# k's mixes: the first product of each moved from VectorE to ScalarE, two behind each sigmoid of r's units 4 and 5

## The chip, the cores and the metric

The kernel runs on the 8 NeuronCores of one Trainium2 chip. Each core takes 1024 of the 8192 tokens (two sequences of 4096, four chunks each), with a lane of 128 tokens ahead of its chunk, and computes all 2048 channels of them. The cores exchange nothing. The metric is the device time of the slowest core, in microseconds.

## The reference, cut to what matters

The layer normalises x, mixes each token with the one before it in four ways, multiplies the mixes by four matrices, runs a recurrence over tokens, multiplies by Wo, normalises again and gates with a second projection whose weights are rounded to -1, 0 or 1.

```python
prev = jnp.concatenate([x[:, 1:2, :], x[:, :-1, :]], axis=1)
xx = prev - x
xk = x + xx * tm_k        # xv, xr, xg likewise
r = xr @ Wr.T;  k = xk @ Wk.T;  v = xv @ Wv.T
g = sigmoid(xg @ Wg.T)
wkv = _wkv_scan(k, v, exp(-exp(time_decay)), time_first)
o = sigmoid(r) * wkv * g @ Wo.T
s = layernorm(o) * ln_g + ln_b
return xn + s * silu(ffn(xn))
```

A mix is computed as xn(now) * (1 - tm) + xn(before) * tm. "The first product" below is xn(now) * (1 - tm); the second instruction multiplies xn(before) by tm and adds the first product.

## The kernel before

Channels lie on partitions, in 16 groups of 128, and tokens along the free axis. `xn` (f16, 16 groups) is the normalised input. `mova` and `movb` (bf16) hold mixes: r's mix is in `mova` first, k's goes into `movb`, and v's overwrites r's in `mova`. A matrix comes in eight units of 256 output channels, loaded into the slots R0, R1, R2, X0 and X1.

Nothing is scheduled automatically. The class `Program` keeps one queue for each engine, written in the order of the code, and each engine runs its queue strictly in that order. `P.op` gives back a token; a later operation that is passed this token waits for it. So what stands ahead in a queue and waits delays all that is behind it in that queue.

The place of the change is the passage from r to k and v:

- TensorE works through r's units 4 and 5 (`unit_tile`, eight tiles of 16 matmuls, 512 columns each), then through units 6 and 7 with the 16 channel groups in the outer loop: for each group `ic`, eight matmuls go into the eight PSUM banks (`bk`). Then come k and v in turns, tile by tile: three tiles of k for one group of output channels, three tiles of v, and so on.
- The counter `turn` is set to 4 ahead of units 4 and 5. Their eight tiles therefore use the banks 4, 5, 6, 7, 0, 1, 2, 3, and the eight accumulations of units 6 and 7 use the same banks in the same order. The first round of units 6 and 7 (`ic` 0) needs each bank emptied: its eighth matmul goes into bank 3, which holds the eighth tile of units 4 and 5.
- ScalarE empties the banks with sigmoids (`sr_evict`), after it has done the sigmoids of r's first four units and two small exponentials.
- VectorE makes k's 16 mixes (`t_kb`), and then v's 16 (`t_va`). A mix over 1152 tokens is two instructions in `lerp`: a TENSOR_SCALAR into the buffer `lu` (two of them, in turns), and a SCALAR_TENSOR_TENSOR out of it. The mix of group `ic` for v may not start before units 6 and 7 have read that group of `mova` (`t_ic[ic]`).
- The first matmul of k waits for all of `t_kb`, the first matmul of v for all of `t_va`.

An existing helper, `lerp_pair`, makes r's mixes with the first product on ScalarE, in pieces of 512 or 256 tokens with four buffers.

Of the kernel before, what the change touches and what calls it, by code (L numbers as in the profile page):

```python
# [9 lines left out]
AF = mybir.ActivationFunctionType  # L10
OP = mybir.AluOpType
# [10 lines left out]
T_ALL = LANE + T_OWN  # L22
# [3 lines left out]
TMK, TMV, TMR, TMG = 0, 1, 2, 3  # L26
# [75 lines left out]
def build_nc():  # L102
    nc = bass.Bass("TRN2", target_bir_lowering=False)
    P = Program(nc)
# [21 lines left out]
    def at(name, shape, dtype, offset):  # L126
        return nc.alloc_sbuf_tensor_at(name, shape, dtype, offset=offset)

    xn = at("xn", [128, CH, 1154], F16, XN)
    mova = at("mova", [128, CH, T_ALL], BF16, A)  # L130
    movb = at("movb", [128, CH, T_ALL], BF16, B)
# [11 lines left out]
    lu = [at("lu0", [128, T_ALL], F16, SMALL), at("lu1", [128, T_ALL], F16, ROWS + 20736)]  # L143
# [26 lines left out]
    def sm(name, n, dtype=F32):  # L170
        nonlocal small
        t = at(name, [128, n], dtype, small)
        small += -(-n * (2 if dtype == F16 else 4) // 32) * 32
        return t
    vec = sm("vec_sb", 161)
    ident = vec[:, 97:161].bitcast(F16)
    om = sm("om", 64)
# [147 lines left out]
    def lerp(dst, ic, tm, col, n, *tokens):  # L325
        k = lu_n[0] % 2
        lu_n[0] += 1
        u = lu[k]
        P.op("DVE", lambda e: e.tensor_scalar(u[:, 0:n], xn[:, ic, col:col + n],
                                              om[:, 16 * tm + ic:16 * tm + ic + 1], None, OP.mult),  # L330
             *tokens)
        return P.op("DVE", lambda e: e.scalar_tensor_tensor(  # L332
            dst, xn[:, ic, col - 1:col - 1 + n], vec[:, 16 * tm + ic:16 * tm + ic + 1], u[:, 0:n],
            OP.mult, OP.add), drain=True)
# [4 lines left out]
    def lerp_pair(dst, ic, tm, col, n, *tokens):  # L339
# [9 lines left out]
            OP.mult, OP.add), t_u, *tokens)  # L349
        return lq_free[k]  # L350


    stg_free = [None] * 6
    nstg = [0]
# [28 lines left out]
    def unit_tile(mat, u, oc, mov, t0, n, *tokens):  # L383

        slot = have[(mat, u)]
        b = next_bank()
        for ic in range(CH):
            tok = mm(ps[b][:, 0:n], unit[slot][:, ic, 128 * oc:128 * oc + 128],
                     mov[:, ic, t0:t0 + n], ic == 0, ic == CH - 1,
                     have[(mat, u, ic // 8)], bank_free[b], *(tokens if ic == 0 else ()),  # L390
                     signal=ic == CH - 1)
        return b, tok


    def sr_evict(b, och, t0, n, tok, c0=0):
        bank_free[b] = P.op("ACT", lambda e: e.activation(
            att[:, och, t0:t0 + n], ps[b][:, c0:c0 + n], AF.Sigmoid), tok)
# [36 lines left out]
    t_om = P.op("DVE", lambda e: e.tensor_scalar(om[:, :], vec[:, 0:64], -1.0, 1.0, OP.mult, OP.add), t_vec)  # L434
# [157 lines left out]
    t_head = [t_xn[(0, 0)], t_xn[(0, 1)], t_xh[(0, 1)]] + xh_free  # L592
    stg_free[1] = t_grp[7]


    t_kb = [lerp(movb[:, ic, :], ic, TMK, 2, T_ALL, *t_head) for ic in range(16)]

    rslot = {3: "X0", 4: "X1", 5: "R0", 6: "R1", 7: "X0"}
    turn[0] = 4
# [3 lines left out]
    for u in (4, 5):  # L603
        for oc in range(2):
            for h in range(2):
                b, tok = unit_tile("wr", u, oc, mova, 512 * h, 512)
                sr_evict(b, 2 * u + oc, 512 * h, 512, tok)
        slot_free[rslot[u]] = tok
    kslot = [("R0", "R2", "R1")[n % 3] for n in range(16)]

# [7 lines left out]
    t_va = []  # L618
    t_ic = []
# [10 lines left out]
    t_rend = t_grp[7]  # L630

    for ic in range(16):
        t_va.append(lerp(mova[:, ic, :], ic, TMV, 2, T_ALL, t_ic[ic]))


    P.op("DVE", lambda e: e.memset(za[:, 0:1], 0.0), t_rend)
# [450 lines left out]
```

How the kernel before makes its waits and increments, by code:

```python
        def run(e):  # L60
            for s, n in todo:
                e.wait_ge(s, n)
            if drain:
                e.drain()
            ins = emit(e)
            if signal:
                ins.then_inc(self.sem[eng], 1)
# [13 lines left out]
        def run(e):  # L81
            for s, v in todo:
                e.wait_ge(s, v)
            if accum_op == OP.bypass:
                e.dma_start(out, in_).then_inc(sem, 16)
            else:
                e.dma_start(out, in_, accum_op=accum_op).then_inc(sem, 16)
# [7 lines left out]
        def run(e):  # L95
            for s, v in todo:
                e.wait_ge(s, v)
```

## Time and profile before

| | us |
|---|---|
| Median of 3 runs (lowest, highest) | 743.63 (743.05, 745.22) |
| The profiled execution's own time | 743.03 |
| Its span on the slowest core (all cores: 739.7 to 741.3) | 741.3 |
| Outside the span | 1.7 |
| TensorE busy in the span | 706.4 (95%) |
| VectorE busy | 465.9 (63%) |
| ScalarE busy | 241.3 (33%) |
| Mean granted TensorE clock, share of full | 0.995 to 0.997 |

The table reads so: TensorE is at work nearly all the time, and the times of the eight cores lie within 1.6 us of each other. The other two engines have a good deal of idle time, averaged over the span, which says nothing yet of any one stretch.

### The profile page before, as it was taken

How to read it: one execution, taken by the hardware profiler on the slowest of the kernel's cores; microseconds unless marked ns; L12 is line 12 of the kernel's file. 1: busy time of each engine (PE TensorE's matmuls, PEld its weight loads, DVE VectorE, ACT ScalarE, POOL GpSimd, SP SyncE). 2: the span in 40 equal slices, each digit the busy share in tenths (PEclk: the TensorE clock that was granted, in tenths of full speed). 3: DMA queues.
4: the chain of work that ended last, by engine and by line, in shares of the span. 5: the costliest groups of instructions: out<-in, count | busy, mean ns of one | idle time of the engine just before them, and what ended most of it. 6: DMA issues, size and time to landing. Idle time of an engine off the chain costs nothing.

```text
span 741.3 us, 10313 instructions; the slowest of 8 cores (739.7 to 741.3 us)
## 1 busy us (share of the span) xinstructions
PE 706.4 (95%) x3809; PEld 372.0 (50%) x3852; DVE 465.9 (63%) x580; ACT 241.3 (33%) x344; POOL 123.8 (17%) x156
## 2 busy tenths in 40 slices
PE   1889999999999999999999999999999999999994
PEld 1447644456666666666665444444444444444441
DVE  6777589957777677776789496674111110566565
ACT  4766751043444234442126654412111110000000
POOL 1010101001010010100000000112134410876710
PEclk9999999999999999999999999999999999999997
DMA  8988194444783958739317933894999975356643
GB/s 237 172 222 171 30 212 85 73 114 90 195 152 95 225 117 209 144 93 217 65 51 199 334 108 78 185 168 36 138 176 149 171 149 158 86 142 156 185 113 113
DMA packets 22372, 107.71 MB, mean 145 GB/s; under 512 B 2482, under 2 KB 2610, under 8 KB 14898
## 3 DMA queue, kind: packets, MB, share of 16 engines
q0 software_dynamic: 12672, 50.34, 41.1%
q1 hardware_dynamic: 9648, 56.71, 24.5%
q8 instruction: 31, 0.51, 0.3%
q14 instruction: 17, 0.14, 0.1%
q10 hardware_dynamic: 4, 0.02, 0.0%
HBM read 140.61 MB, written 8.39 MB: 201 GB/s over the span
## 4 chain that ended last, share of the span: by engine, by line
PE 83%; DVEq 5%; DMA 5%; DVE 4%; issue 1%; ACT 1%; POOL 0%; ACTq 0%; SPq 0%; POOLq 0%
PE ps L380 83%; DVEq L64 5%; DVE movb L332 3%; DMA wR<-wr 3%; DMA xs<-x 2%; PE ps L290 1%; DVE mova L332 0%; DVE zt L966 0%; ACT xh L268 0%; DVE bst L245 0%; DVE ps L960 0%; POOL wR L85 0%; DVE xn L317 0%; ACT raw L400 0%; DVE bst L952 0%
## 5 line engine op out<-in xcount | busy, mean ns | idle before, releaser
L380 PE MATMUL ps<-mova,wR 128*128 128x384 bf16 (+2 forms) x1555 | 283.4, 340 | 5.2 <-DMA wR<-wr 3.0
L380 PEld LDWEIGHTS ps<-mova,wR 128*128 128x128 bf16 x1568 | 152.6, 98 | 130.3 <-issue 7.7
L380 PE MATMUL ps<-movb,wR 128*128 128x384 bf16 x768 | 127.4, 326 | 0.0
L380 PE MATMUL ps<-wo,att 128*128 128x512 bf16 x502 | 110.1, 379 | 0.5
L380 PE MATMUL ps<-wq,xn 128*128 128x512 bf16 x501 | 109.9, 379 | 0.7
L380 PEld LDWEIGHTS ps<-movb,wR 128*128 128x128 bf16 x768 | 75.1, 98 | 49.7
L380 PEld LDWEIGHTS ps<-wo,att 128*128 128x128 bf16 x512 | 50.1, 98 | 60.4
L380 PEld LDWEIGHTS ps<-wq,xn 128*128 128x128 f16 x512 | 50.0, 98 | 60.5 <-issue 0.3
L868 DVE TENSOR_TENSOR att<-sg,att 128x512 bf16<-128x512 bf16 x32 | 15.2, 475 | 96.1 <-ACT sg L866 96.1
L711 DVE TENSOR_TENSOR kv<-ps,ek 128x384 f32<-128x384 f32 x48 | 26.6, 557 | 51.4 <-PE ps L380 47.9
L952 DVE BATCH_NORM_STATS2 bst<-ps 128x6 f32<-128x512 f32 x32 | 21.4, 691 | 46.4 <-PE ps L380 46.4
L866 ACT ACTIVATE sg<-ps 128x512 bf16<-128x512 f32 x32 | 19.1, 597 | 87.3 <-PE ps L380 87.3
L332 DVE SCALAR_TENSOR_TENSOR mova<-xn,vec_sb,lu 128x1152 bf16<-128x1152 f16 (+2 forms) x33 | 44.0, 1333 | 3.1
L645 ACT ACTIVATE ek<-ps,hb 128x128 f32<-128x128 f32 x16 | 5.9, 367 | 120.2 <-PE ps L380 120.2
L380 PE MATMUL ps<-mova,wX 128*128 128x512 bf16 x186 | 43.9, 379 | 0.3
L657 DVE TENSOR_TENSOR_SCAN zb<-w_sb,ek 128x1152 f32<-128x1152 f32 x16 | 40.9, 2559 | 1.5
L672 DVE TENSOR_TENSOR_SCAN za<-w_sb,kv 128x1152 f32<-128x1152 f32 x16 | 40.9, 2559 | 1.4
L702 ACT ACTIVATE wq<-stg,nmag 128x2048 bf16<-128x2048 f32 x16 | 31.4, 1996 | 21.5 <-DVE stg L700 21.5
L776 DVE SCALAR_TENSOR_TENSOR ps<-ps,nscale,bias 128x512 f32<-128x512 f32 x32 | 24.2, 757 | 20.5 <-PE ps L380 19.2
L85 POOL DMA_DIRECT2D wR<-wv x16 | 8.5, 536 | 157.4 <-PE ps L380 157.4
L955 ACT ACTIVATE sd<-mv,eps 128x1 f32<-128x1 f32 x8 | 2.4, 294 | 93.4 <-DVE mv L954 93.4
L780 ACT ACTIVATE g<-ps 128x512 bf16<-128x512 f32 x32 | 18.7, 597 | 39.7 <-DVE ps L776 39.5
(83 smaller groups left out, 638.9 us busy)
## 6 DMA issues: line engine op xcount, KB each, us to landing
stg<-wf SPq DMA_DIRECT2D x32, 1024.0 KB, 9.1
xs<-x SPq DMA_DIRECT2D x9, 1024.0 KB, 9.3
wR<-wk POOLq DMA_DIRECT2D x16, 512.0 KB, 11.0
wR<-wv POOLq DMA_DIRECT2D x16, 512.0 KB, 10.7
wo<-wo POOLq DMA_DIRECT2D x16, 512.0 KB, 23.7
y<-zt SPq DMA_DIRECT2D x7, 1024.0 KB, 7.2
wR<-wg POOLq DMA_DIRECT2D x12, 512.0 KB, 17.2
stg<-x POOLq DMA_DIRECT2D x6, 1024.0 KB, 9.4
```

What stands on the lines that cost most here:

```text
L64: e.drain()
L332: return P.op("DVE", lambda e: e.scalar_tensor_tensor(dst, xn[:, ic, col - 1:col - 1 + n], vec[:, 16 * tm + ic:16 * tm + ic + 1], u[:, 0:n ...
L380: return P.op("PE", lambda e: e.matmul(bank, w_ap, m_ap, start=first, stop=last), *tokens, signal=signal)
L657: P.op("DVE", lambda e: e.tensor_tensor_scan(zb[:, 1:1 + T_ALL], wb, ek[m][:, :], 0.0, OP.mult, OP.add), t_weu, drain=True)
L672: P.op("DVE", lambda e: e.tensor_tensor_scan(za[:, 1:1 + T_ALL], wb, kv[:, :], 0.0, OP.mult, OP.add), drain=True)
L702: t_wq[(s, q)] = P.op("ACT", lambda e: e.activation(dst, stg[i][:, :], AF.Sign, bias=nmag[:, 0:1]), t, t_nmag, wq_free[s % 2], *tokens)
L711: bank_free[b] = P.op("DVE", lambda e, j=j, b=b: e.tensor_tensor(kv[:, 384 * j:384 * j + 384], ps[b][:, 0:384], ek[m][:, 384 * j:384 * j + ...
L776: t = P.op("DVE", lambda e: e.scalar_tensor_tensor(ps[b][:, :], ps[b][:, :], nscale[:, 0:1], bias[s % 2][:, :], OP.mult, OP.add), tok, t_b ...
L780: bank_free[b] = P.op("ACT", lambda e: e.activation(g2[s][:, tb, :], ps[b][:, :], AF.Silu), t, t_att[15] if s >= 2 else None)
L866: t = P.op("ACT", lambda e: e.activation(sg[k][:, :], ps[b][:, :], AF.Sigmoid), tok, sg_free[k])
L868: sg_free[k] = P.op("DVE", lambda e: e.tensor_tensor(att[:, och, 512 * h:512 * h + 512], sg[k][:, :], att[:, och, 512 * h:512 * h + 512], ...
L952: P.op("DVE", lambda e, s=s: e.bn_stats(bst[m][:, 6 * s:6 * s + 6], ps[banks[s]][:, :]), toks[s])
```

## The change

A new helper `lerp_wide` makes a mix over all 1152 tokens with its first product on ScalarE (an ACTIVATE Copy with a scale per partition) and its second instruction on VectorE. It uses the whole of both `lu` buffers, in turns by `ic % 2`; the first product of group `ic` waits until VectorE has finished the mix of group `ic - 2`. The first two of k's mixes are written ahead of units 4 and 5; the other fourteen stand in pairs behind the first seven of the eight sigmoids of units 4 and 5. v's first mix waits, in addition, until both buffers are free.

```diff
+    lw_free = [None] * 2
+
+    def lerp_wide(dst, ic, tm, *tokens):
+
+        k = ic % 2
+        t_u = P.op("ACT", lambda e: e.activation(lu[k][:, :], xn[:, ic, 2:2 + T_ALL], AF.Copy,
+                                                 scale=om[:, 16 * tm + ic:16 * tm + ic + 1]),
+                   t_om, lw_free[k], *tokens)
+        lw_free[k] = P.op("DVE", lambda e: e.scalar_tensor_tensor(
+            dst, xn[:, ic, 1:1 + T_ALL], vec[:, 16 * tm + ic:16 * tm + ic + 1], lu[k][:, :],
+            OP.mult, OP.add), t_u, *tokens)
+        return lw_free[k]
...
-    t_kb = [lerp(movb[:, ic, :], ic, TMK, 2, T_ALL, *t_head) for ic in range(16)]
+    t_kb = [lerp_wide(movb[:, ic, :], ic, TMK, *t_head) for ic in range(2)]
...
                 sr_evict(b, 2 * u + oc, 512 * h, 512, tok)
+                for ic in range(len(t_kb), min(len(t_kb) + 2, 16)):
+                    t_kb.append(lerp_wide(movb[:, ic, :], ic, TMK))
...
     for ic in range(16):
-        t_va.append(lerp(mova[:, ic, :], ic, TMV, 2, T_ALL, t_ic[ic]))
+        t_va.append(lerp(mova[:, ic, :], ic, TMV, 2, T_ALL, t_ic[ic], *(lw_free if ic == 0 else ())))
```

On ScalarE, in the kernel before, the last small exponential (into `eu_sb`) is followed directly by the sigmoids that empty the banks of units 4 and 5, one bank (`ps4`, `ps5`, ...) after the other; the number behind `ps` is the bank:

```order
L591 ACTIVATE eu_sb_123<-vec_sb_120 128x16
L396 ACTIVATE att_46<-ps4 128x512 [waits done_PE]
L396 ACTIVATE att_46<-ps5 128x512 [waits done_PE]
L396 ACTIVATE att_46<-ps6 128x512 [waits done_PE]
L396 ACTIVATE att_46<-ps7 128x512 [waits done_PE]
```

In the changed kernel two first products (L357, into `lu0` and `lu1`) stand between each two of them. These are the last rows of the eight, up to the sigmoid of bank 3, which is the eighth; the sigmoid of `ps4` behind it is already one of units 6 and 7:

```order
L357 ACTIVATE lu0_62<-xn_43,om_121 128x1152 [waits done_DVE]
L357 ACTIVATE lu1_63<-xn_43,om_121 128x1152 [waits done_DVE]
L409 ACTIVATE att_46<-ps2 128x512 [waits done_PE]
L357 ACTIVATE lu0_62<-xn_43,om_121 128x1152 [waits done_DVE]
L357 ACTIVATE lu1_63<-xn_43,om_121 128x1152 [waits done_DVE]
L409 ACTIVATE att_46<-ps3 128x512 [waits done_PE]
L409 ACTIVATE att_46<-ps4 128x512 [waits done_PE]
```

All sixteen first products of k now stand ahead of the sigmoid of bank 3 in ScalarE's queue, and each of them but the first two waits for VectorE.

On VectorE, at the end of k's mixes and the start of v's, the kernel before has pairs without waits on another engine:

```order
L329 TENSOR_SCALAR lu_62<-xn,om 128x1152
L332 SCALAR_TENSOR_TENSOR movb<-xn,vec_sb,lu_62 128x1152
L329 TENSOR_SCALAR lu_63<-xn,om 128x1152
L332 SCALAR_TENSOR_TENSOR movb<-xn,vec_sb,lu_63 128x1152
L329 TENSOR_SCALAR lu_62<-xn,om 128x1152 [waits done_PE]
```

In the changed kernel the second instructions of k (L360) are alone and wait for ScalarE, and v's first mix also waits for VectorE's own last one:

```order
L360 SCALAR_TENSOR_TENSOR movb<-xn,vec_sb,lu_62 128x1152 [waits done_ACT]
L360 SCALAR_TENSOR_TENSOR movb<-xn,vec_sb,lu_63 128x1152 [waits done_ACT]
L329 TENSOR_SCALAR lu_62<-xn,om 128x1152 [waits done_PE,done_DVE]
L332 SCALAR_TENSOR_TENSOR mova<-xn,vec_sb,lu_62 128x1152
L329 TENSOR_SCALAR lu_63<-xn,om 128x1152 [waits done_PE]
```

Sixteen instructions have left VectorE's queue here. TensorE's, GpSimd's and the DMA queues hold the same instructions in the same order as before.

## Rows read from the trace of the kernel before

**Rows 1.** TensorE's waits over the span: engine, line waited for, total us, times, longest.

```profile
PE ps L380 <- DVE zb L637: 0.5, 1, 0.5
```

**Rows 2.** Chain that ended last, in order of time: start us, us, what.

```profile
156.05 1.42 DVE mova L332
157.61 210.76 PE ps L380 x1296
```

**Rows 3.** Timeline of VectorE, 95 to 157 us: start, us, instruction, idle before it.

```profile
95.22 0.52 DVE L329 TENSOR_SCALAR lu<-xn,om 128x1152 f16<-128x1152 f16 x1 [0.18 <-DVE xn L317]
...
97.16 0.51 DVE L329 TENSOR_SCALAR lu<-xn,om 128x1152 f16<-128x1152 f16 x1
...
124.99 1.42 DVE L332 SCALAR_TENSOR_TENSOR movb<-xn,vec_sb,lu 128x1152 bf16<-128x1152 f16 x1
126.33 0.52 DVE L329 TENSOR_SCALAR lu<-xn,om 128x1152 f16<-128x1152 f16 x1
...
156.05 1.42 DVE L332 SCALAR_TENSOR_TENSOR mova<-xn,vec_sb,lu 128x1152 bf16<-128x1152 f16 x1
```

**Rows 4.** Timeline of ScalarE, 100 to 122 us.

```profile
100.39 0.20 ACT L591 ACTIVATE eu_sb<-vec_sb 128x16 f32<-128x16 f32 x1
100.60 1.28 ACT L396 ACT_TABLE_LOAD   x1
101.90 1.08 ACT L396 ACTIVATE att<-ps 128x512 bf16<-128x512 f32 x2
104.55 0.60 ACT L396 ACTIVATE att<-ps 128x512 bf16<-128x512 f32 x1 [1.56 <-PE ps L380]
...
121.81 0.60 ACT L396 ACTIVATE att<-ps 128x512 bf16<-128x512 f32 x1 [2.86 <-PE ps L380]
```

**Rows 5.** Timeline of TensorE, 122 to 158 us.

```profile
122.42 1.03 PE L380 MATMUL ps<-mova,wX 128*128 128x512 bf16 x4
...
149.18 7.96 PE L380 MATMUL ps<-movb,wR 128*128 128x384 bf16 x48
157.61 7.64 PE L380 MATMUL ps<-mova,wR 128*128 128x384 bf16 x46 [0.47 <-DVE zb L637]
```

**Rows 6.** ScalarE's groups of instructions by shape: busy us, mean ns of one.

```profile
L663 ACT ACTIVATE ek<-ek 128x1024 f32<-128x1024 f32 x16 | 16.9, 1058 | 1.3
...
L344 ACT ACTIVATE lu<-xn,om 128x256 f16<-128x256 f16 x32 | 13.2, 497 | 2.8 <-DVE xn L317 2.8
...
L344 ACT ACTIVATE lu<-xn,om 128x512 f16<-128x512 f16 x15 | 9.4, 709 | 3.6 <-DVE xn L317 3.6
L268 ACT ACTIVATE xh<-xs,nm,rs 128x1024 f16<-128x1024 f32 x6 | 7.1, 1233 | 2.1 <-DVE nm L263 1.3 <-DVE om L434 0.7
...
L226 ACT ACT_TABLE_LOAD x1 | 1.3, 1283 | 1.7 <-DVE ones L225 1.7
```

**Rows 7.** Timeline of ScalarE: two series of one instruction, back to back.

```profile
75.73 5.68 ACT L344 ACTIVATE lu<-xn,om 128x256 f16<-128x256 f16 x14
...
147.93 4.03 ACT L396 ACTIVATE att<-ps 128x512 bf16<-128x512 f32 x8 [25.52 <-PE ps L380]
```

**Rows 8.** Timelines: hand-overs between VectorE and ScalarE, and from ScalarE to TensorE.

```profile
34.08 0.69 DVE L317 COPY xn<-ps 128x1024 f16<-128x1024 f16 x1
34.86 3.79 ACT L344 ACTIVATE lu<-xn,om 128x512 f16<-128x512 f16 x6 [2.78 <-DVE xn L317]
35.75 2.74 DVE L347 SCALAR_TENSOR_TENSOR mova<-xn,vec_sb,lu 128x512 bf16<-128x512 f16 x4 [0.99 <-ACT lu L344]
...
55.40 0.59 ACT L400 ACTIVATE raw<-ps 128x512 f32<-128x512 f32 x1
...
56.13 4.09 PE L380 MATMUL ps<-mova,wR 128*128 128x256 bf16 x34 [0.22 <-ACT raw L400]
```

**Rows 9.** Busy time by stretch (PE, PEld, DVE, ACT, POOL), granted clock, DMA share.

```profile
121.00:157.00 36.00, 35.84 (x177) 17.33 (x178) 34.29 (x37) 7.04 (x13) 3.58 (x6) 1.00 0.52 85
```

**Rows 10.** Timeline of TensorE after its longest wait before 93 us.

```profile
46.17 3.61 PE L380 MATMUL ps<-mova,wR 128*128 128x512 bf16 x16 [1.81 <-DMA wR<-wr]
```

## The prediction

> **What bounds the kernel now.** I read TensorE's waits first, because it is busy for 706.4 of 741.3 us. The line that matters is the only one that names the mixes of k and v: TensorE waits once for VectorE there, 0.5 us in all [rows 1]. Then the chain that ended last, and here a reader has to be careful. It runs through VectorE's mixes up to 157.47 us and then through TensorE for 210 us without a break [rows 2], which looks as if all 62 us of mixes set the time. But the timeline of TensorE shows it at work beside them: units 6 and 7 from before 122.42, k from 149.18 to 157.14, and only then a gap of 0.47 us before v's first matmul at 157.61 [rows 5]. In the stretch from 121 to 157 us it is busy for 35.84 of 36.00 us at a granted clock of 1.00, the 2.4 GHz level [rows 9]. So the most that any speeding up of these mixes can give is 0.47 us; what it can cost is not limited like that. VectorE needs 1.94 us for a mix (95.22 to 97.16) and is through with k at 126.41 and with v at 157.47 [rows 3]. ScalarE empties a bank every 3.45 us and idles between: it waits 2.86 us for TensorE ahead of the eighth sigmoid, which runs from 121.81 to 122.41 [rows 4].
>
> **The change part by part.**
>
> *What goes from VectorE.* Sixteen TENSOR_SCALAR of 0.52 us, which start 0.61 ahead of their partners: k's mixes would take 1.34 us each instead of 1.94 (a following instruction starts 1.34 after a SCALAR_TENSOR_TENSOR of 1.42, 124.99 to 126.33 [rows 3]), 9.6 us less, if ScalarE kept up.
>
> *What comes to ScalarE.* A Copy over 1152 elements has no row. The same instruction takes 709 ns for 512 elements and 497 ns for 256 [rows 6], 0.83 ns for each further one, so 1.24 us for 1152. From both sides: the shortest 1024-element row (1.058) gives 1.16 with 128 elements more, the longest (1.233, an ACTIVATE with per-partition operands) 1.34. I take 1.24, since it is the same form. One back to back with the next starts 0.095 before the end: fourteen of 497 ns take 5.68, so 0.399 apart; for sigmoids it is (4.03 - 0.60) / 7 = 0.49 apart [rows 7].
>
> *The hand-overs.* VectorE's copy ends at 34.77 and ScalarE starts at 34.86: 0.09. That product ends at 35.57 and VectorE starts at 35.75: 0.18. ScalarE's eviction ends at 55.99 and TensorE's matmul starts at 56.13: 0.14 [rows 8]. For the bounds I give both of the first two the lower or the higher value. With two buffers, a product waits for the mix two back. So from one product to the second after it there are at least 1.24 + 0.18 + 1.42 + 0.09 = 2.93 us. ScalarE's own work for a pair and a sigmoid is 2 x 1.145 + 0.49 = 2.78, VectorE's 2 x 1.34 = 2.68. The loop through both buffers is the longest: a pair takes 2.93 us.
>
> *ScalarE's queue, step by step.* It is free at 100.60, where the load of the sigmoid's table now stands [rows 4]. Products 0 and 1 start at 100.60 and 101.74; the second ends at 102.98. The table load then puts the first sigmoid 1.30 later (100.60 to 101.90 in [rows 4]), at 104.29. Product 2 starts at 104.78 and 3 at 105.92. The mix of 2 starts at 106.20 and that of 3 behind it at 107.54, to 108.96, so product 5 starts at 109.05. Five loops of 2.93 take product 15 to 123.70. The eighth sigmoid is behind it: 124.85 to 125.45. No other sigmoid is late for anybody: the seventh stands one pair earlier, ends at about 122.5 with bank 2, and TensorE wants that bank at 122.85.
>
> *Who waits for the eighth sigmoid.* It empties bank 3. Units 6 and 7 write the banks in turn, and the row at 122.42 holds the fifth to eighth matmul of their first round, 0.217 apart [rows 5]: the eighth starts at 122.42 + 3 x 0.217 = 123.07. Now the bank is free only at 125.45, and with 0.14 of hand-over the matmul starts at 125.59. Behind it, in TensorE's own order, stands everything else. **TensorE stalls for 2.52 us**, where it did not before.
>
> *What gives some of it back.* k's mixes end at about 126.6 (product 15 ends at 124.94, 0.18 of hand-over, 1.42, and a little queueing behind the mix before). v's first then starts 0.18 later, because it waits for VectorE's own last result, as the first one of k does [rows 3]: 126.8 against 126.33. v's mixes follow 1.94 apart and end at 157.9 instead of 157.47; they gain nothing, because k's are paced by ScalarE. But TensorE now comes to v at 157.14 + 2.52 = 159.66, so the 0.47 us wait goes, with 1.7 us to spare. The matmuls of units 6 and 7, 1.73 us a group, run ahead of v's mixes as before. The 9.6 us taken off VectorE turn into waits of VectorE for ScalarE.
>
> *The sum.* 2.52 - 0.47 = **+2.05 us**. Behind this point the chain is TensorE alone [rows 2], so nothing absorbs it. On the profiled execution's own 743.03 it gives 745.1; the median of the three runs lies 0.60 above that execution, and on it I predict **745.7**. By the bounds: with 1.16 and 0.09 twice the loop is 2.76, the eighth sigmoid ends at 124.2, and the sum is +0.8. With 1.34 and 0.18 twice the loop is 3.12, the sigmoid ends at 126.9, and the sum is +3.5.
>
> *A page weighed against a row.* What the table load costs decides when everything behind it starts, and rows show 1.30 us from its start to that of the sigmoid. The Trainium skill, "ScalarE: Activation LUTs", section "What ACT_TABLE_LOAD costs", puts a switch at about 2.66 us, the load and a drain of about 1.38. By that page the sum would be about +3.4; this trace disagrees with it at this very load, 1.30.
>
> **The rivals.**
>
> 1. *No stall; only the gain.* If the first products are so quick that the eighth sigmoid is done by 122.93, the 0.47 us wait goes for nothing: 743.2. The backlog would have to be 2.5 us shorter over seven pairs, 2.57 us a pair, which is under VectorE's own 2.68. The rows speak against it.
>
> 2. *A shorter or longer stall by the price of the product.* 744.4 at the low bound, 747.1 at the high one; from +2.2 on it counts as slower.
>
> 3. *The load is followed by a wait until the long products have drained.* Before the load there were tiny instructions in this place. A second 1.30 us, the load's own length once more, makes +3.35: 747.0. This is what the page named above would have; the rows speak against it.
>
> 4. *TensorE's clock falls in the stall.* After its wait of 1.81 us it ran sixteen matmuls in 3.61 us, 0.215 apart, at the full level [rows 10], but it has no wait of 2.5 us behind such a busy stretch. If the granted clock went to 1.2 GHz for as long as those sixteen take, they would need 3.5 us more: 749.2. The point from which it decides is a stall longer than the one that the rows show to be harmless.
>
> 5. *Each product loads a table of its own, and each sigmoid loads its table again.* Two loads of 1.30 for each pair: the eighth sigmoid some 18 to 20 us later, 764. Against it: r's mixes did 47 such Copies among square roots, and the only load in that stretch is the one at the start [rows 6]. The Trainium skill, in the same page's section on table sets, says that a copy is in every set, and the trace agrees: no load among those 47.
>
> **How the numbers follow.** The forecast, a stall that makes +1.4 to +2.8, gets 0.62. A longer one (+2.8 to +3.7) gets 0.15, a shorter one (+0.5 to +1.4) 0.12, no stall 0.05, and the drain, the clock and the reloads 0.02 each. A measurement of this kernel can tell about 0.3% from no change, 2.23 us or 745.86. That line lies just above my forecast. Of the forecast's 0.62 I put 0.26 above it; with 0.15 and 0.06 that is 0.47 for slower. Nothing in this stretch has 2.2 us to give, so faster gets 0.01; the rest, 0.52, is the same. The range is 744.1 to 747.3: the two bounds, 0.3 us wider on each side since single runs of the kernel differ by more than 2 us, and it leaves out no stall, the clock and the reloads.
>
> **What would show it.** In the changed profile: ScalarE busy without pause from 94 to about 125.4 us; products of 1.24 us; a pair every 2.93; exactly one table load between 100 and 148; TensorE's wait of 2.5 us for ScalarE, in the row that starts at about 125.6, within the first round of units 6 and 7; no wait ahead of v; VectorE's mixes of k with waits for ScalarE, and v's starting at 126.8. I am wrong if the eighth sigmoid ends before 123 us (products much cheaper than 1.16), if the granted clock is under 1.00 after the stall, or if TensorE waits at k or v again.

## The result, and the profile after

| | us |
|---|---|
| Kernel before, median (lowest) | 743.92 (743.05) |
| Changed kernel, median (lowest) | 746.38 (745.91) |
| Ratio, 95% interval | 1.0036 (1.0026 to 1.0046) |
| Profiled execution after: own time, span on core 5 | 746.6, 745.0 |
| Spans of the cores after | 741.4 to 745.0 |

The kernel is slower by 0.36% in the ratio, 2.46 us between the medians; forecast were 745.7 and +2.05. (Executions in which one die ran at a lower clock throughout, one of the changed kernel's eight, count in the medians but not in the ratios, nor where cores are counted below.)

TensorE's waits in the changed kernel, on its slowest core, are these; against [rows 1], the wait for VectorE is gone and one for ScalarE has come:

```profile
PE ps L393 <- DMA wR<-wr: 3.2, 2, 2.4
PE ps L393 <- ACT att L409: 2.1, 1, 2.1
```

The timeline of ScalarE in the changed kernel answers to [rows 4]. Products and sigmoids follow one another without idle time, with one table load:

```profile
100.88 0.20 ACT L604 ACTIVATE eu_sb<-vec_sb 128x16 f32<-128x16 f32 x1
100.98 2.40 ACT L357 ACTIVATE lu<-xn,om 128x1152 f16<-128x1152 f16 x2
103.40 1.28 ACT L409 ACT_TABLE_LOAD   x1
104.69 0.60 ACT L409 ACTIVATE att<-ps 128x512 bf16<-128x512 f32 x1
105.19 2.39 ACT L357 ACTIVATE lu<-xn,om 128x1152 f16<-128x1152 f16 x2
107.48 0.58 ACT L409 ACTIVATE att<-ps 128x512 bf16<-128x512 f32 x1
108.05 2.58 ACT L357 ACTIVATE lu<-xn,om 128x1152 f16<-128x1152 f16 x2
110.54 0.58 ACT L409 ACTIVATE att<-ps 128x512 bf16<-128x512 f32 x1
...
122.67 2.48 ACT L357 ACTIVATE lu<-xn,om 128x1152 f16<-128x1152 f16 x2
125.06 0.58 ACT L409 ACTIVATE att<-ps 128x512 bf16<-128x512 f32 x1
```

The timeline of TensorE on the same core answers to [rows 5]; its first row, from an earlier stage, is used further down:

```profile
46.66 3.61 PE L393 MATMUL ps<-mova,wR 128*128 128x512 bf16 x16 [2.35 <-DMA wR<-wr]
...
122.91 0.81 PE L393 MATMUL ps<-mova,wX 128*128 128x512 bf16 x3
125.78 0.38 PE L393 MATMUL ps<-mova,wX 128*128 128x512 bf16 x1 [2.06 <-ACT att L409]
126.00 1.02 PE L393 MATMUL ps<-mova,wR 128*128 128x512 bf16 x4
126.86 1.68 PE L393 MATMUL ps<-mova,wX 128*128 128x512 bf16 x4
128.33 1.91 PE L393 MATMUL ps<-mova,wR 128*128 128x512 bf16 x4
130.04 1.26 PE L393 MATMUL ps<-mova,wX 128*128 128x512 bf16 x4
131.14 1.03 PE L393 MATMUL ps<-mova,wR 128*128 128x512 bf16 x4
...
153.58 7.96 PE L393 MATMUL ps<-movb,wR 128*128 128x384 bf16 x48
161.38 7.96 PE L393 MATMUL ps<-mova,wR 128*128 128x384 bf16 x48
```

Two losses are to be seen. The first is the predicted one: the row at 122.42 held four matmuls before; at 122.91 there are three, and the fourth, due at 122.91 + 3 x 0.217 = 123.56, starts at 125.78. That is 2.22 us. The second I had not reckoned with: four matmuls that took 0.86 us from start to start (126.00 to 126.86) take 1.71 a little later (128.33 to 130.04), 0.43 us each, which is half the rate. The stretches of this core show the granted clock of it (the third number from the end):

```profile
121.00:126.00 5.00, 2.94 (x14) 1.18 (x13) 4.73 (x4) 4.61 (x5) 2.12 (x4) 1.00 0.10 13
126.00:130.00 4.00, 4.00 (x13) 1.52 (x12) 3.71 (x5) 0.00 (x0) 0.00 (x0) 0.64 1.04 176
130.00:140.00 10.00, 10.00 (x47) 4.50 (x46) 8.97 (x11) 0.00 (x0) 0.00 (x0) 0.97 0.80 135
```

The clock went to its lower level, 1.2 GHz, behind the stall and came back. Over 121 to 140 us it is 0.91 on cores 0, 1 and 4 to 7, and 1.00 on cores 2 and 3, where the same stall stands. On core 3:

```profile
122.34 0.81 PE L393 MATMUL ps<-mova,wX 128*128 128x512 bf16 x3
125.21 0.38 PE L393 MATMUL ps<-mova,wX 128*128 128x512 bf16 x1 [2.06 <-ACT att L409]
125.43 1.02 PE L393 MATMUL ps<-mova,wR 128*128 128x512 bf16 x4
126.29 1.03 PE L393 MATMUL ps<-mova,wX 128*128 128x512 bf16 x4
```

To compare cores and kernels free of how they began, I use one length below, which I call **the passage**: from the fifth matmul of the first round of units 6 and 7 (the row with wX) to v's first matmul. Before, it is 157.61 - 122.42 = 35.19 us on core 6, and 35.19 to 35.22 on all eight. After, it is 159.13 - 122.34 = 36.79 us on core 3 (v's first matmul at 159.13), **+1.60**, and 161.38 - 122.91 = 38.47 on core 5, **+3.28**. The difference of 1.68 us is the clock. The metric is the slowest core. In each of seven executions of the changed kernel, 3 to 6 of the eight cores had a mean clock below 0.9945, and the slowest core was one of them; in the profiled execution before no core was (0.995 to 0.997), and of the 55 executions of the kernel before that are counted beside the experiments, 31 had none, 20 had one and four had more. That mean is a blunt sign of a fall in this passage: in the profile of e2_stall_22 below, six cores fell and only three have a mean below 0.9945, and a core can also fall elsewhere (last section).

The terms of the passage and the time do not agree to the end: a core whose clock fell has +3.28, the medians differ by 2.46 and the lowest times by 2.86. Two things in the record can make the difference. The cores come to the passage at 120.67 to 122.91 us, and which of them falls differs from one execution to the next, so the latest core need not be one that fell; and the median before, 743.92, is 0.3 to 0.5 above that of the same kernel in the experiments. How much each is worth, nothing here shows.

### The profile page after: what moved, and what is told of

It is laid out like the page before. It is cut to its first block, busy times and chain, and to the rows that moved or that the text cites. A ratio compares the mean times of both kernels' runs of the same rounds, so it can differ in the third digit from the quotient of the medians.

```text
span 745.0 us, 10373 instructions; the slowest of 8 cores (741.4 to 745.0 us)
## 1 busy us (share of the span) xinstructions
PE 710.8 (95%) x3852; PEld 372.9 (50%) x3852; DVE 459.9 (62%) x564; ACT 259.6 (35%) x360; POOL 123.4 (17%) x156
## 4 chain that ended last, share of the span: by engine, by line
PE 88%; DMA 5%; ACT 3%; issue 2%; DVE 1%; DVEq 0%; POOL 0%; ACTq 0%; SPq 0%; POOLq 0%
PE ps L393 87%; DMA wR<-wr 3%; DMA xs<-x 3%; ACT lu L357 1%; ACT att L416 1%; ACT att L409 0%; PE ps L290 0%; DVE zt L981 0%; ACT xh L268 0%; DVEq L64 0%; DVE ps L975 0%; ACT L602 0%; POOL wR L85 0%; ACT raw L413 0%; DVE bst L967 0%
## 5 line engine op out<-in xcount | busy, mean ns | idle before, releaser
L883 DVE TENSOR_TENSOR att<-sg,att 128x512 bf16<-128x512 bf16 x32 | 16.7, 522 | 94.2 <-ACT sg L881 94.2
L393 PE MATMUL ps<-mova,wX 128*128 128x512 bf16 x192 | 45.9, 384 | 2.1 <-ACT att L409 2.1
```

What stands on the lines that cost most here:

```text
L393: return P.op("PE", lambda e: e.matmul(bank, w_ap, m_ap, start=first, stop=last), *tokens, signal=signal)
L883: sg_free[k] = P.op("DVE", lambda e: e.tensor_tensor(att[:, och, 512 * h:512 * h + 512], sg[k][:, :], att[:, och, 512 * h:512 * h + 512], ...
```

## The experiments

All were timed beside the kernel before on their own chip, whose median was 743.45 us for the first four and 743.66 for the last four. The medians are of 6 to 12 executions. Stall, cores and passage are from one profiled execution of each kernel; the cores are those of eight whose clock fell within the passage.

| kernel | stall, us | cores whose clock fell | passage, us | median, us | ratio, 95% interval |
|---|---|---|---|---|---|
| before | 0 | 0 | 35.19 | | |
| changed | 2.22 | 6 | 36.79 or 38.47 | 746.38 | 1.0036 (1.0026 to 1.0046) |
| e1_sigmoids_ahead | 0 | 0 | 35.89 | 743.55 | 0.9989 (0.9966 to 1.0012) |
| e2_stall_22 | 2.22 | 6 | 36.79 or 38.47 | 746.30 | 1.0029 (1.0006 to 1.0052) |
| e3_stall_11 | 1.08 | 0 | 35.64 | 743.99 | 0.9996 (0.9974 to 1.0018) |
| e4_three_buffers | 1.27 | 0 | 35.83 | 743.67 | 0.9995 (0.9974 to 1.0015) |
| e5_bank3_later | 0 | 0 | 35.52 | 743.25 | 0.9995 (0.9985 to 1.0005) |
| e6_stall_32 | 3.47 | 8 | 39.5 to 41.0 | 748.71 | 1.0062 (1.0044 to 1.0079) |
| e7_six_on_scalar | 0 | 0 | 34.57 | 742.75 | 0.9996 (0.9980 to 1.0011) |
| e8_stall_16 | 1.62 | 0 | 36.18 | 744.23 | 1.0009 (0.9996 to 1.0023) |

My theory at this point: TensorE waits for the eighth sigmoid, and the fallen clock follows from that wait. The rival: ScalarE's load, or the waits and the order on VectorE, cost something of their own.

**The sigmoids ahead of the products.**

```diff
-    t_kb = [lerp_wide(movb[:, ic, :], ic, TMK, *t_head) for ic in range(2)]
+    t_kb = [lerp_wide(movb[:, ic, :], ic, TMK, *t_head) for ic in range(0)]
...
-                    t_kb.append(lerp_wide(movb[:, ic, :], ic, TMK))
+                    t_kb.append(lerp_wide(movb[:, ic, :], ic, TMK, *(t_head if ic == 0 else ())))
```

> All sixteen first products stay on ScalarE, but none stands ahead of the first sigmoid and the last pair stands behind the eighth. Theory (the only loss is TensorE's wait for the eighth sigmoid, and the fallen clock follows from that wait): the eighth sigmoid ends at about 123.0 us instead of 125.6, TensorE's wait in the first round of units 6 and 7 shrinks from 2.2 us to 0.2 or less, the granted clock stays 1.00 on all cores, and as k's mixes end at about 127 us, v's wait comes back, 1 to 1.4 us instead of the 0.6 before. Sum against the kernel before: +0.5 to +1.0 us. Rival (it is the load of ScalarE or the order on VectorE as such that costs): it stays at +2.5 us, and the clock falls here too.

ScalarE does the same sixteen products, and its eighth sigmoid now stands one pair earlier. Its timeline:

```profile
119.85 2.49 ACT L357 ACTIVATE lu<-xn,om 128x1152 f16<-128x1152 f16 x2
122.25 0.58 ACT L409 ACTIVATE att<-ps 128x512 bf16<-128x512 f32 x1
122.72 2.57 ACT L357 ACTIVATE lu<-xn,om 128x1152 f16<-128x1152 f16 x2
```

TensorE's, on the same core:

```profile
122.33 1.03 PE L393 MATMUL ps<-mova,wX 128*128 128x512 bf16 x4
...
158.22 0.97 PE L393 MATMUL ps<-mova,wR 128*128 128x384 bf16 x5 [1.17 <-DVE zb L652]
```

The four matmuls stand together again, the granted clock is 1.00 on all cores from 121 to 134 us, and v waits 1.17 us for VectorE, all as expected. The passage is +0.70 us, all of it v's longer wait. The median moved by 0.10, under the +0.5 to +1.0 on record, but the interval of the ratio reaches from -2.5 to +0.9 us, so the time settles nothing between them. The rival's +2.5 us with a fallen clock is refuted: position alone, with all the products kept, removes the stall and the fall.

**The stall alone.** The kernel before, with ScalarE held up ahead of the eighth sigmoid by Copies that change nothing.

```diff
+                if (u, oc, h) == (5, 1, 1):
+                    for c, n in enumerate((1024, 1024, 384)):
+                        P.op("ACT", lambda e, c=c, n=n: e.activation(att[:, c, 0:n], att[:, c, 0:n], AF.Copy),
+                             tok, drain=True)
                 sr_evict(b, 2 * u + oc, 512 * h, 512, tok)
```

> The kernel before, all mixes on VectorE, with three Copies of parts of att onto themselves ahead of the eighth sigmoid of units 4 and 5, so that it ends some 2.7 us later. The result is not changed. Theory: TensorE stalls by 2.2 us as in the changed kernel, the granted clock falls on most cores to half for 3 to 4 us (1.7 us lost), v's wait of 0.6 us goes: the same time as the changed kernel, +2.4 to +2.9 us. Rival (products on ScalarE and VectorE's waits have a cost of their own): clearly less than the changed kernel, at most +1.6, and no fall of the clock.

The timeline of TensorE on its slowest core:

```profile
123.98 0.81 PE L380 MATMUL ps<-mova,wX 128*128 128x512 bf16 x3
126.85 0.38 PE L380 MATMUL ps<-mova,wX 128*128 128x512 bf16 x1 [2.06 <-ACT att L396]
...
162.45 2.76 PE L380 MATMUL ps<-mova,wR 128*128 128x384 bf16 x16
```

The stall is the same to a hundredth, six cores again lose their clock (0.91 over 121 to 140 us), and the passage is 38.47 us with the fall and 36.79 without it (cores 6 and 7): the changed kernel's numbers, with every mix still on VectorE. The median is +2.85 us. So the stall and what follows from it are the whole of the loss. (Core 2, the slowest here, had lost its clock once already, behind a wait of 2.10 us for weights at 46.05; its passage is not touched by that.)

**How long a stall the clock bears.** The same edit with other lengths of Copies: `(1024, 384)`, `(1024, 1024)` and `(1024, 1024, 1024, 512)`.

> As e2_stall_22 with Copies for half the delay; the result is not changed. Theory (the clock falls only when the stall is long): stall 1.1 us, granted clock 1.00 on all eight cores, v's wait of 0.6 us gone: +0.5 us. Rival (any stall at this place drops the clock): +1.5 to +2.2 us with several cores under 1.00.

> As e2_stall_22 with Copies that give a stall of about 1.65 us; the result is not changed. Theory (between 1.1 us, where no core lost its clock, and 2.2 us, where six did): few or no cores fall; +1.0 us where none does, up to +2.0 in runs in which one does. Rival: as many cores fall as at 2.2 us and the median is +2.3 us.

> As e2_stall_22 with longer Copies: a stall of 3.3 us; the result is not changed. Theory: the clock falls on all eight cores, and each loses 1.7 us or a little more: +4.2 to +4.8 us. Rival (the fall is chance and does not depend on the length of the stall): some cores stay at 1.00 and the median is near +3.5.

In the passage, at 1.08 and at 1.62 us no core of the profiled execution fell; at 2.22 six of eight did; at 3.47 all eight. Without a fall the passage is 34.57 us plus the stall each time (35.64, 36.18, 36.79). At 3.47 us, 34.57 + 3.47 = 38.04; six cores have 39.5 to 39.7, 1.4 to 1.7 more, but two have 40.8 and 41.0, 2.8 to 2.9 more, with a granted clock of 0.82 instead of 0.91 over 121 to 140 us. This is core 1:

```profile
121.00:140.00 19.00, 15.69 (x60) 6.31 (x59) 15.36 (x17) 3.48 (x5) 1.97 (x4) 0.82 0.69 112
```

I had expected 1.7 us or a little more for the fall, and a stall of 3.3: the passage of the last two cores is 1.1 us more than that price allows. The median of +5.05 lies above the +4.2 to +4.8 on record, but it rests on six executions and the interval of the ratio, +3.3 to +5.9 us, holds both. For the stalls of 1.08 and 1.62 us the passage is +0.45 and +0.99 (on record +0.5 and +1.0), which the times cannot tell from no change.

**A third buffer.** It tests what sets ScalarE's pace.

```diff
-    lw_free = [None] * 2
+    lw_free = [None] * 3
+    lw = lu + [at("lu2", [128, T_ALL], F16, ROWS + 16384)]
...
-        k = ic % 2
+        k = ic % 3
```

> The changed kernel with a third buffer for the first products, so that a product waits for the mix three back. Theory (the loop through two buffers sets the pace, 2.93 us a pair): the pace becomes ScalarE's own 2.79 us, the eighth sigmoid comes 0.85 us earlier, the stall is 1.3 to 1.4 us instead of 2.2, fewer cores lose their clock: +0.8 us without the fall, up to +1.5 with it. Rival (ScalarE's own work sets the pace already): the pace stays at 2.93 and the time at +2.5 us.

The timeline of ScalarE:

```profile
107.16 0.58 ACT L410 ACTIVATE att<-ps 128x512 bf16<-128x512 f32 x1
...
123.78 0.60 ACT L410 ACTIVATE att<-ps 128x512 bf16<-128x512 f32 x1
```

Six pairs in 16.62 us are 2.77 us each, where the changed kernel has (125.06 - 107.48) / 6 = 2.93. The pace was set by the loop through two buffers, as the prediction had it, and is now set by ScalarE's own work. The stall falls from 2.22 to 1.27 us, no clock falls, and the passage is +0.64; on record were 1.3 to 1.4 and +0.8. The rival's 2.93 did not hold.

**TensorE's own order.** ScalarE and VectorE as in the changed kernel; only the matmuls into bank 3 of groups 0 and 1 go to the end of the third round.

```diff
+        todo = [(ic, j) for j in range(7 if ic < 2 else 8)]
+        if ic == 2:
+            todo += [(0, 7), (1, 7)]
+            todo.remove((2, 7))
+            todo.append((2, 7))
+        for g, j in todo:
```

> The changed kernel, with ScalarE's and VectorE's queues as they are; only TensorE's first rounds of units 6 and 7 are rewritten: the matmuls of groups 0 and 1 into bank 3 stand at the end of the third round. Theory (the stall is nothing but the order of that one matmul ahead of others that could run): TensorE has no wait there, the granted clock stays 1.00 on all cores, and since v's mixes still begin at about 126.9 us, v's wait is 1.2 us: +0.5 to +0.8 us against the kernel before, and 2 us less than the changed kernel. Rival (TensorE is held up by ScalarE's load in other ways too): the time stays above +1.5 us.

There is no stall and no fallen clock, but v's wait is 0.80 us and not 1.2. VectorE's timeline:

```profile
126.28 0.52 DVE L329 TENSOR_SCALAR lu<-xn,om 128x1152 f16<-128x1152 f16 x1 [0.39 <-PE ps L393]
```

On this core v's first mix starts 4.23 us into the passage (which begins at 122.05), and in the changed kernel 126.87 - 122.91 = 3.96. I had taken the 126.9 of one core for the time of all. The 0.39 us of waiting for TensorE is the edit's own doing: v's first mix overwrites group 0 of `mova`, which is now read to the end only by the matmul moved to the third round. In the changed kernel the mix starts 0.11 us after the one before it (126.76 to 126.87), so an estimated 0.28 us of v's wait comes from this. What the times of VectorE would be without it, the run doesn't show. The passage is +0.33 instead of +0.5 to +0.8. What it was made for it shows all the same: the stall is one matmul that stands ahead of others that could run.

**Only as many products as ScalarE has room for.** Six of the sixteen on ScalarE, one behind each of the first six sigmoids; ten mixes stay on VectorE. The six go through one buffer, the ten through the other and a third one.

```diff
+    t_kb = [own(ic) for ic in range(4)]
+    wide = {0: (4,), 1: (6,), 2: (8,), 3: (10,), 4: (12,), 5: (15,)}
+    behind = {0: (5,), 1: (7,), 2: (9,), 3: (11,), 4: (13, 14), 5: ()}
...
                 sr_evict(b, 2 * u + oc, 512 * h, 512, tok)
+                for ic in wide.get(nsr, ()):
+                    t_kb.append(wide_end(ic, wide_product(ic)))
+                t_kb += [own(ic) for ic in behind.get(nsr, ())]
```

> Six of k's sixteen first products on ScalarE, one behind each of the first six sigmoids of units 4 and 5; ten mixes stay whole on VectorE, four of them before the first. Theory: ScalarE keeps pace with TensorE (1.6 us of work for each 3.45), the eighth sigmoid stays where it was before, k's mixes end at about 122.7 us, v's start at 123.6 as soon as the first group of mova is free, and v's wait of 0.6 us goes: -0.6 us, with no wait of TensorE between 93 and 160 us. Rival (v's mixes end late for another reason): v's wait stays, and no change.

The timeline of ScalarE on core 4:

```profile
119.70 0.58 ACT L396 ACTIVATE att<-ps 128x512 bf16<-128x512 f32 x1
122.02 0.60 ACT L396 ACTIVATE att<-ps 128x512 bf16<-128x512 f32 x1 [1.74 <-PE ps L380]
```

And of TensorE:

```profile
122.62 1.03 PE L380 MATMUL ps<-mova,wX 128*128 128x512 bf16 x4
...
157.19 3.09 PE L380 MATMUL ps<-mova,wR 128*128 128x384 bf16 x18
```

The eighth sigmoid waits for TensorE again and not the other way round. No core has a wait of TensorE between 93 and 170 us, and the passage is 34.56 or 34.57 us on all eight, 0.62 less than before. That is all that there was to gain. The medians differ by 0.91 us, but the interval of the ratio holds 1: the traces show the gain, the times alone do not. In the profiled execution seven cores have spans of 738.5 to 741.1 us; core 6 has 744.2, having come to the passage 3 us later than core 4 (125.94 to 160.51, the same 34.57 us). What it lost lies at 46.91, where it waited 3.17 us for weights and its clock fell (the row stands in the last section); the change has no part in it.

## Why the prediction was right, and where it was not

**The bound and the place.** Right. The mixes that looked critical in the chain could give only TensorE's short wait at v, and the loss came at the first matmul into bank 3, behind ScalarE's eighth sigmoid. The two opposite experiments, the stall without the products and the products without the stall, show it.

**The products and the pace.** The groups by shape of the changed kernel, beside [rows 6], have the new Copy:

```profile
L357 ACT ACTIVATE lu<-xn,om 128x1152 f16<-128x1152 f16 x16 | 19.8, 1249 | 0.2
```

Right, then: 1.249 us against 1.24, 2.93 us a pair on average, the loop through two buffers, one table load. What the Trainium skill ("ScalarE: Activation LUTs", "What ACT_TABLE_LOAD costs") says of about 2.66 us for a switch is not borne out here either: behind two long products it is 1.29 us from the load's start to the sigmoid's (103.40 to 104.69).

**The size of the stall.** 2.52 us forecast, 2.22 measured. Of the 0.30, 0.10 is the first product, which starts 0.10 before the exponential's end (100.98 against 100.88 + 0.20) where I started it behind that end. The other 0.2 is the series from the second sigmoid to the eighth: 17.58 us (107.48 to 125.06), and 17.78 by my steps (product 3 starts at 105.92, so that sigmoid is at 107.07, and the eighth at 124.85). Most of that is the loop: its last five turns take (125.06 - 110.54) / 5 = 2.90 us each, not 2.93.

**What is given back.** 0.47 us forecast, 0.63 measured. I took the idle time in the row, which counts from the modelled end of the last matmul. From start to start, k's 48 matmuls take 7.80 us (153.58 to 161.38), so before, v could have begun at 149.18 + 7.80 = 156.98, 0.63 ahead of 157.61. The passage of 34.57 in the last experiment shows the same 0.62. The sum without the clock should have been 2.22 - 0.63 = 1.59, and the two cores that kept their clock have +1.60.

**The clock.** This is the step that failed: the sum had the clock at nothing. The rival had a chance of 0.02, on the ground that a wait of 1.81 us had done no harm [rows 10]; and its price, 3.5 us, was taken from a length that I had chosen. Six of eight cores fell, at 1.68 us each, and a slowest-core metric needs only one. Counted as that row counts it, as idle time, the stall is 2.06 us, only 0.25 more; a single harmless wait on one core bounds nothing beyond its own length. The sign that I had named for being wrong, a granted clock under 1.00 after the stall, is there, 0.64 on core 5 over 126 to 130 us.

**The time.** Predicted 745.7, measured 746.38 with the kernel before at 743.92; it lies in a range that was said to leave the clock out. That is partly luck. The terms of the sum were 0.45 us too high (+2.05 where a core without a fall has +1.60), and the clock that was missing from it adds 1.68 where it falls, +3.28 together. The time that was measured, +2.46, lies between the two and so near the forecast, for the reasons given with the passage, of which the prediction had none. With that, the slower side, at 0.47, was underrated.

## What to carry to other kernels

Before work is put on an engine that is idle on average, look for whoever waits for that engine's next short instruction: here it was a PSUM bank that TensorE needed back 0.7 us after the sigmoid's old end (123.07 against 122.41), and sixteen products of 1.25 us stood ahead of it. Put the instruction that frees a resource ahead of the filler, and give only as much filler as the period holds: the first alone took the stall away and still left the passage 0.70 us longer than before, the second made it 0.62 shorter. And when a change makes TensorE stall, price the stall and what its clock does afterwards as two terms, on the slowest core.

## What the runs showed of the hardware

At the place of the change, a stall of TensorE cost more than its length from somewhere between 1.6 and 2.2 us on: no core of eight fell to the lower clock at 1.08, 1.27 or 1.62 us, six did at 2.22 (in two different kernels), and all at 3.47, in one profiled execution each. At 2.22 us each fall cost 1.68 us; at 3.47 six cores lost 1.4 to 1.7 and two 2.8 to 2.9.

The same happened far ahead of the change, where TensorE waits for weights or for r's mixes. By the idle time that the rows give, the stalls above are 0.92, 1.11, 1.46, 2.06 and 3.30 us. Core 1 of e3_stall_11, core 2 of e2_stall_22 and core 6 of e7_six_on_scalar:

```profile
31.65 18.68 PE L380 MATMUL ps<-mova,wR 128*128 128x512 bf16 x78 [2.47 <-ACT lu L344]
...
46.05 5.30 PE L380 MATMUL ps<-mova,wR 128*128 128x512 bf16 x16 [2.10 <-DMA wR<-wr]
...
46.91 6.40 PE L380 MATMUL ps<-mova,wR 128*128 128x512 bf16 x16 [3.17 <-DMA wR<-wr]
```

Sixteen such matmuls take 3.61 us at the full clock, and the 78 took 17.00 on core 7 of the kernel before. So the falls cost 1.68 us after 2.47, 1.69 after 2.10 and 2.79 after 3.17: the prices of the passage again, though neither the changed instructions nor the sigmoid are near. A fall of this kind may be behind the slower executions of the kernel before, with 745 to 746 us; none of those was profiled.

Length alone does not decide it. On core 5 of the changed kernel, TensorE had waited 2.35 us earlier on and ran at full rate behind it, 16 matmuls in 3.61 us (the row at 46.66 in its timeline above), and two cores of eight kept their clock after 2.06. Why some cores fall and others do not after the same wait stays open; I ran nothing that would tell it.

The two rates themselves are 0.43 us a matmul of 512 columns in the fallen stretch and 0.216 outside it. The Trainium skill ("TensorE: Matmul & The Clock Gate", "Wait — 56ns, not 53.3ns?") gives 426.7 and 215.7 ns, and the trace agrees.
